# A four-layer network in one kernel: a new order of PE's work in the state-space loop, early weights for the layer behind it, and four rounds of the last attention's values moved to the sorted sparse layer's tail

## What is computed

```python
x = x + L0_xattn(ctx, layernorm(x))     # state-space scan, see below
x = x + L0_ffn(layernorm(x))            # sparse, 8 experts of which 2, and a shared one
x = x + L1_xattn(layernorm(x), ctx)
x = x + L1_ffn(layernorm(x))
x = x + L2_xattn(layernorm(x), ctx)
x = x + L2_ffn(layernorm(x))            # attention, then a sparse layer of 8 experts, sorted
x = x + L3_xattn(layernorm(x), ctx)     # 16 heads of 128; keys ctx @ Wk, values ctx @ Wv
x = x + L3_ffn(layernorm(x))
```

```python
def step(state, inp):
    d, b, c, u = inp
    dA = jnp.exp(d[..., None] * A)
    state = state * dA + (d * u)[..., None] * b[:, None, :]
    y = jnp.einsum('bdn,bn->bd', state, c)
    return (state, y)
```

```python
k = (encoder_hidden_states @ Wk).reshape(B, Skv, H, D)
v = (encoder_hidden_states @ Wv).reshape(B, Skv, H, D)
k = rmsnorm(k, gk)
```

## Time and profile before

| | |
|---|---|
| median of 3 runs | 1465.5 us (1464.37 to 1468.17) |
| the profiled execution | 1465.39 us, span 1463.5 us |
| busy, share of the span | PE 1312.8 us (90%), DVE 1022.4 (70%), ACT 707.2 (48%), POOL 270.1 (18%) |
| mean granted clock of PE | 0.947 of full speed |
| the loop of 32 steps | 41.5 to 184.1 us |
| the rest of `mamba` and the seam to `ffn0`'s first matmul | 184.1 to 204.3 us |
| blocks of `moe3` | 862 to 984.4 us |
| head of `attn4` up to its first transposes | 987.8 to 1001.0 us |

### The profile page before, as it was taken

One profiled execution on the slowest core, in us unless ns is written; L12 is line 12 of the kernel. 1 busy time (PEld: TensorE's weight loads), 2 busy tenths in 40 slices (PEclk: granted clock), 3 DMA queues, 4 the chain that ended last, 5 costly groups with the idle time before them and its releaser, 6 DMA issues.

```text
span 1463.5 us, 20903 instructions
## 1 busy us (share of the span) xinstructions
PE 1312.8 (90%) x6697; PEld 917.8 (63%) x6697; DVE 1022.4 (70%) x2266; ACT 707.2 (48%) x1824; POOL 270.1 (18%) x256
## 2 busy tenths in 40 slices
PE   7788869989998667999999799995999999989998
PEld 4354445555333244676667589984888888765555
DVE  7888777889896787887788623235666666667665
ACT  5777613443775665555554212223666666633111
POOL 0666520000000002222121173121111111201000
PEclk8899979999999769999999799997999999979999
DMA  6476640015430200000004198855222222102230
GB/s 224 153 221 214 218 180 0 1 23 94 70 56 2 83 0 1 1 37 1 37 1 131 33 348 320 305 192 180 99 72 72 72 72 72 36 1 48 79 93 29
DMA packets 82434, 141.53 MB, mean 97 GB/s; under 512 B 45493, under 2 KB 56958, under 8 KB 77008
## 3 DMA queue, kind: packets, MB, share of 16 engines
q1 hardware_dynamic: 80480, 136.28, 29.6%
q0 software_dynamic: 1872, 4.22, 0.8%
HBM read 105.06 MB, written 26.37 MB: 90 GB/s over the span
## 4 chain that ended last, share of the span: by engine, by line
PE 67%; DVE 10%; ACT 3%; issue 2%; DMA 2%; POOL 1%; SPq 0%; DVEq 0%; ACTq 0%; POOLq 0%
PE psum L3295 5%; PE psum L2496 5%; PE psum L2068 4%; PE psum L958 4%; PE psum L2792 4%; PE psum L2844 4%; PE psum L2822 4%; PE psum L2110 4%; PE psum L2857 3%; PE psum L3305 3%; PE psum L2507 2%; DVE roomB L1624 2%; PE psum L2100 2%; PE psum L2800 2%; PE psum L992 2%
## 5 line engine op out<-in xcount | busy, mean ns | idle before, releaser
L2914 ACT ACTIVATE roomA<-psum,roomA 128x256 f32<-128x256 f32 x128 | 70.9, 559 | 87.4 <-DVE roomA L2981 86.9
L2165 ACT ACTIVATE roomA<-psum,roomA 128x128 f32<-128x128 f32 (+1 forms) x128 | 53.2, 426 | 84.4 <-DVE roomA L2240 84.2
L1624 DVE TENSOR_REDUCE roomB<-psum 128x2 f32<-128x512 f32 x128 | 81.4, 686 | 8.8 <-PE psum L1463 8.2
L2031 POOL TENSOR_TENSOR roomA<-roomA 128x512 f32<-128x512 f32 x40 | 50.8, 1270 | 177.0 <-DVE roomA L2233 177.0
L875 POOL TENSOR_TENSOR roomA<-roomA 128x1024 f32<-128x1024 f32 (+1 forms) x32 | 74.5, 2328 | 48.3 <-PE psum L596 31.4
L530 PE MATMUL psum<-roomB,own 128*128 128x256 f32 x256 | 69.6, 402 | 15.2 <-ACT roomB L632 14.7
L2644 DVE SCALAR_TENSOR_TENSOR roomA<-roomA,psum 128x512 f32<-128x512 f32 x23 | 15.9, 690 | 95.5 <-ACT roomA L2543 89.4
L2068 PE MATMUL psum<-own,roomB 128*128 128x512 f32 x160 | 75.0, 594 | 3.4 <-DVE roomA L2232 2.1
L530 PEld LDWEIGHTS psum<-roomB,own 128*128 128x128 f32 x256 | 48.1, 196 | 46.1 <-ACT roomB L632 26.0
L3295 PE MATMUL psum<-roomA,roomB 128*112 128x512 f32 (+1 forms) x168 | 74.8, 593 | 0.3 <-DVE roomA L3523 0.3
L796 DVE TENSOR_TENSOR_SCAN roomA<-roomA,psum 128x512 f32<-128x512 f32 x64 | 74.4, 1204 | 0.0
(11 more groups left out here) (520 smaller groups left out, 3325.3 us busy)
## 6 DMA issues: line engine op xcount, KB each, us to landing
roomB<-m_w_dram SPq DMA_DIRECT2D x12, 1536.0 KB
roomA<-m_w_dram SPq DMA_DIRECT2D x11, 1536.0 KB
a_kv_ready<-roomB SPq DMA_DIRECT2D x32, 512.0 KB, 3.6
roomA<-m_c_rows SPq DMA_DIRECT2D x32, 512.0 KB, 4.8
roomA<-a_kv_ready SPq DMA_DIRECT2D x8, 1024.0 KB, 4.8
roomA<-a_kv_ready SPq DMA_DIRECT2D x16, 512.0 KB, 4.3
roomB<-a_w_dram SPq DMA_DIRECT2D x4, 1280.0 KB, 6.0
roomB<-f_w_dram SPq DMA_DIRECT2D x8, 624.0 KB, 4.0
```

The costliest lines, as they stand in the source:

```text
L1624: dve.tensor_reduce(maxneg[:, hp // 8, :, m, hp % 8], g.bank(m).rearrange("p (q k) -> p q k", k=S), AX.X, ALU.max, negate=True).then_inc(s ...
```

## The change

In `mamba`, the rounds in the loop fall from 26 to 22: 28 of the 32 rounds are left (`ROUNDS`), and the last four of values, pairs 6 and 7 of the heads, go to `moe3`. The steps with a round are 1 to 28 without 5, 9, 13, 17, 21 and 25. In a step PE now runs `spread`, the second half of the round that the step before began, the `add`, and then the first half of its own round. ACT's squares of a key round are cut in two fours, one behind the copy and one in the next step, behind the decay and ahead of the next copy. SP's stores come a step later. PE's last `add` stands ahead of `back(0)`. The buffer of the squares moves, so that the room from word 1200 on is free for the weights of `ffn0`; these are cut into ten loads (gate, six pieces of up, three of down), one in each step from 14 to 23, behind the row load and the store.

In `moe3`, SP loads the weights of the four late rounds with the small tables (several of the layer's semaphores are joined in one), and behind the last down matmuls PE runs the four rounds, each of four matmuls, ACT copies each and issues its store itself. The first two rounds wait for the last block's hidden values, the other two for the copies of the first two. SP waits for the four stores ahead of `attn4`'s loop.

```diff
@@ mamba
-    k_sq, k_tmp = rb.take(8, P), rb.take(3, 16 * NT)
-    rb.at = 10200
+    assert rb.at <= 1200
+    rb.at = 9176
+    k_sq = rb.take(8, P)
...
-    IN_LOOP = 32 - AHEAD
+    ROUNDS, WEIGHTS_AT = 32 - LATE_V, 14
+    IN_LOOP = ROUNDS - AHEAD
...
-    values = list(range(AHEAD)) + [AHEAD + i for i in range(IN_LOOP) if i % 13 in (1, 4, 6, 9, 11)]
-    keys = [r for r in range(32) if r not in values]
+    values = list(range(AHEAD)) + [AHEAD + i for i in range(IN_LOOP) if i % 11 in (2, 6, 9)]
+    keys = [r for r in range(ROUNDS) if r not in values]
...
             if 3 <= k + 2 < STEPS:
                 row(k + 2)
-            if k - 1 in round_at:
-                keep(round_at[k - 1])
+            if k - 2 in round_at:
+                keep(round_at[k - 2])
+            if 0 <= k - WEIGHTS_AT < g.f0_parts:
+                g.f0_part(sp, k - WEIGHTS_AT)
...
             if k + 1 < STEPS:
                 spread(k + 1)
-            if k in round_at:
-                kv_round(round_at[k], range(0, 2))
+            if k - 1 in round_at:
+                kv_round(round_at[k - 1], range(2, 4))
             if k:
                 add(k - 1)
             if k in round_at:
-                kv_round(round_at[k], range(2, 4))
-        pe.wait_ge(s["m_kv_copied"], 32)
+                kv_round(round_at[k], range(0, 2))
+        add(STEPS - 1)
+        pe.wait_ge(s["m_kv_copied"], ROUNDS)
         pe.wait_ge(s["m_products"], 2 * STEPS)
         back(0)
-        add(STEPS - 1)
         back(1)
...
+            if k - 2 in round_at and kind_of[round_at[k - 2]] == 0:
+                squares(round_at[k - 2], 1)
             if k - 1 in round_at:
-                r = round_at[k - 1]
-                kv_out(r)
-                if kind_of[r] == 0:
-                    squares(r)
+                kv_out(round_at[k - 1])
+                if kind_of[round_at[k - 1]] == 0:
+                    squares(round_at[k - 1], 0)
@@ ffn0
+    pieces = [(w_gate, d["f0_gate"])]
+    pieces += [(w_up[:, kt, e:e + 3], d["f0_up"][:, kt, e:e + 3]) for kt in range(KD) for e in range(0, E, 3)]
+    pieces += [(w_down[:, e:e + 3], d["f0_down"][:, e:e + 3]) for e in range(0, E, 3)]
+    g.f0_parts = len(pieces)
+    g.f0_part = lambda sp, i: sp.dma_start(*pieces[i]).then_inc(s["f0_weights"], 16)
...
-        sp.dma_start(w_gate, d["f0_gate"]).then_inc(s["f0_weights"], 16)
         keys.sync(sp)
-        for kt in range(KD):
-            sp.dma_start(w_up[:, kt], d["f0_up"][:, kt]).then_inc(s["f0_weights"], 16)
-        sp.dma_start(w_down, d["f0_down"]).then_inc(s["f0_weights"], 16)
...
-        pe.wait_ge(s["f0_weights"], 64)
+        pe.wait_ge(s["f0_weights"], 16 * g.f0_parts)
@@ moe3
+LATE_V = 4
...
+        sp.dma_start(v_late, d["a4_kv"].rearrange("p (n k) c -> p n k c", k=2)[:, 8 - LATE_V // 2:, 1]).then_inc(s["m3_small"], 16)
         ahead["sync"](sp)
...
+        def late_values(r):
+            if r < 2:
+                pe.wait_ge(s["m3_h"], NB)
+            else:
+                pe.wait_ge(s["m3_y"], NB + r - 1)
+            for i in range(4):
+                t = 4 * (r % 2) + i
+                ins = pe.matmul(g.ps[:, (4 + 2 * (r % 2)) * HALF + i * 2 * P:(4 + 2 * (r % 2)) * HALF + (i + 1) * 2 * P],
+                                g.CT[:, t * P:(t + 1) * P], v_late[:, r // 2, :], start=True, stop=True)
+            ins.then_inc(s["m3_up"], 1)
...
             down(b)
+        for r in range(LATE_V):
+            late_values(r)
...
+    def late_values_out(act):
+        for r in range(LATE_V):
+            act.wait_ge(s["m3_up"], NB + r + 1)
+            src = g.ps[:, (4 + 2 * (r % 2)) * HALF:(6 + 2 * (r % 2)) * HALF].rearrange("p (i q c) -> p q i c", i=4, q=2)
+            act.copy(v_staged[r % 4].rearrange("p q (i c) -> p q i c", i=4), src).then_inc(s["m3_y"], 1)
+            act.wait_ge(s["m3_y"], NB + r + 1)
+            act.dma_start(g.kv[8 - LATE_V // 2 + r // 2, 1, :, :, r % 2 * HALF:(r % 2 + 1) * HALF], v_staged[r % 4])\
+               .then_inc(s["m3_v_stored"], 16)
@@ attn4
         g.f5_first(sp)
+        sp.wait_ge(s["m3_v_stored"], 16 * LATE_V)
```

More of the change, by code:

```diff
@@ L632, in kv_out, with squares @@
             act.copy(staged[:, r % 4].rearrange("p q (i c) -> p q i c", i=4), src).then_inc(s["m_kv_copied"], 1)
-        def squares(r):
+        def squares(r, q):
             pair, half = divmod(place_of[r], 2)
@@ L2382, in moe3 @@
     v, u, hot = kept.take(NH, 2, NT), kept.take(NH, NT), kept.take(NH, NT, P)
+    v_late = kept.take(LATE_V // 2, 2 * P)
+    spare = Room(room.tensor, room.size)
+    spare.at = 17600
+    v_staged = hot.rearrange("p h i n -> p (h i n)").rearrange("p (k q t) -> p k q t", k=3, q=2)
+    v_staged = [v_staged[:, k] for k in range(3)] + [spare.take(2, HALF)]
     ahead = ffn5_ahead(g)
```

49 lines of the change are left out of this document (24 added, 25 removed).

## The result

| | before | with the change |
|---|---|---|
| median (range, runs) | 1464.93 us (1463.31 to 1468.17, 4) | 1444.28 us (1441.37 to 1446.41, 4) |
| ratio to before, 95% interval | | 0.9855 (0.9831 to 0.9879) |
| the profiled execution, span | 1465.39 us, 1463.5 | 1444.38 us, 1442.7 |
| mean granted clock of PE | 0.947 | 0.948 |

The change makes the kernel 20.7 us faster; 1442.5 had been forecast, in a range of 1436.5 to 1453. The same program run again later, beside a before of 1464.80 us, took 1446.44 (ratio 0.9874, 0.9859 to 0.9889), 18.4 us less. So 18 to 21 us is what can be said.

The account below looks back on a forecast made before the run. PE's order was taken to bound the loop where it waits, with DVE's own work the floor. From 1465.4 us: - 22.4 (loop) - 1.0 (loop's end) - 1.0 (seam) + 1.5 (tail) = 1442.5 us, range 1436.5 to 1453.

Parts of the forecast that it names:

- The loop: State-space loop: PE's new order and fewer rounds gain 22.4 us of at most 26.9, leaving 4.5; bounds 12 and 26.9.
- the heavy steps at the start: Early in the loop: three steps in a row at 3.87 us leave DVE idle 3 x 0.45 = 1.35 us.
- the balanced groups up to step 16: In the loop, PE and DVE balance within 0.1 us per four steps; small gaps of issue leave 1.0 us idle.
- The end of the loop: Last add ahead of the first half's transposes: DVE's 2.12 us wait shortens, 1.0 us gained, bounds 0.8 and 1.1.
- The early weights: Ten loads, 3.6 MB, in steps 14 to 23: a backlog of 0 to 2.4 us fits; cost 0, bounds 0 and 5.
- The seam: Into the first sparse layer: PE starts at 203.2 instead of 204.2, 1.0 us gained, bounds 0 and 1.0.
- The tail: Sorted sparse layer's end: ACT's four 512 KB stores beside the eight loads of the sums lose 1.5 us.
- ACT as the bound: Rival, 15%: in the loop, 4.49 us of ACT work per key step keeps some 12 us idle; 1450 us.
- DMA as the bound: Rival, 12%: DMA engines bound steps 14 to 23, 38.4 to 41.4 us of work for 39; five more us, 1447.5.
- Stores that cost 5.1: Rival, 10%: in the sorted layer's tail the stores hold back the sums, 5.1 us instead of 1.5; 1446 us.
- Late rows: Rival, 2%: loop rows land late, POOL, add and DVE wait; slower from landings of about 11 us, 1491 at 13.
- Order without effect: Rival, 2%: in the loop DVE waits for something behind `spread`, such as POOL's product; only seams and tail count, 1465.

Follow-up runs that it names:

- the third experiment: Changed kernel with the first sparse layer's weights loaded behind the loop in four pieces, as before: 1447.09 us, ratio 0.9872, loop 120.73 us against 120.96.
- the sixth: Changed kernel with one more 384 KB DRAM-to-DRAM copy beside each piece of weights in steps 14 to 23: 1448.67 us, loop 122.57 us.
- the seventh: Changed kernel with two more 384 KB DRAM-to-DRAM copies beside each piece of weights in steps 14 to 23: 1464.32 us in a single execution, loop 136.68 us.
- the ninth kernel: Changed kernel with nine throwaway matmuls of 512 columns behind the state-space layer's last transpose: 1439.46 us, ratio 0.9837.
- the fourth kernel: Changed kernel with the late rounds' four stores issued by SP behind its eight loads of the sums, not by ACT: 1441.87 us, later 1445.58.

## Why the prediction was right, and where it was not

**The loop: 22.4 forecast, 21.6 measured.** The reading of the timeline held: PE's order was the bound, the copy's wait went, a full step costs PE 3.88 us, and DVE is the bound now. The idle time that stays was put at 3.8 us (4.5 with the stretched steps) and is 4.15. Inside this sum the terms are off in both directions, and that the total came out is partly luck: the first wait is 1.03 us instead of 0.4 (0.57 to 1.91 in the six profiles of this loop; it was longest where the granted clock was still 0.50 until 54 us); the heavy steps at the start 1.77 (0.35, 0.54 and 0.88) instead of 1.35; the balanced groups up to step 16 leave 0.4 instead of 1.0; steps 14 to 17 0.30 instead of 1.0; behind the gates 0.65 where 0 stood. The idle time fell by 20.6 us, so that the steps' own stretch gave 1.0 us, where I had put 1.4 (2.1 less 0.7). In the second profile of the changed kernel the loop is 121.99 us, a gain of 20.6.

**The end of the loop: 1.0 forecast, 0.9 measured**, by the mechanism described.

**The early weights: 0 in the loop was right**, and the third experiment shows it. I argued from a backlog of 0 to 2.4 us; the sixth shows that there was more room than that, about one more piece a step. The queues moved 329 GB/s at a share of 0.99, and 381 when given more, and not the 309 that I had worked out from a stretch at a share of 0.69. Row landings of 5 to 7.4 us came as forecast: 5.5 in the median, and 4.3 without the weights. That POOL waits once they exceed 7.4 is borne out by the sixth and the seventh.

**The seam: 1.0 forecast as a gain, 0.1 measured as a loss in the profile of the result. This step was too simple.** "At the seam PE starts at 203.2 instead of 204.2" took two things as fixed: that the last transposed copy keeps its place, and that what is gained at the first gate matmul is kept. Measured from the last addition to X, the copy ends 11.37 us behind instead of 10.96, so the start gained 0.5; and PE, at half its clock throughout, then took 6.97 us for the gates, where the later start before had caught a stretch at 0.80 (203 to 207 us). The row that hinted at it was in front of me: a clock of 0.67 in the seam. I read it for the bandwidth alone.

One profile cannot price this piece. In the second profile of the changed kernel the gates took 4.89 us and the mark is 29.24, a gain of 1.8 and not a loss. Over all profiles without the throwaway matmuls the mark is 29.2 to 31.2 in the eight with early weights (mean 30.2) and 31.1 to 31.7 in the four with late ones (mean 31.3). So the early weights gave about 1.1 us in the mean; that this is near the forecast of 1.0 is luck, since it holds a varying clock that the forecast left out. PE's clock is worth 1.6 to 3.5 us of the seam, as the ninth kernel shows; the 8.7 us in which DVE makes the norm stay.

**The tail: 1.5 lost forecast, 1.3 measured**, and the fourth kernel takes it back. The mechanism has a part that I did not name: not only are the data's transfers shared, SP's issues themselves slow down.

**The rivals.** ACT as the bound: not with the split squares, 2.8 to 3.9 us of it with whole ones. DMA as the bound: no. Stores that cost 5.1: no. Late rows: not here, but one to two pieces a step away. Order without effect: no.

**The sum** asked for a span of 1463.5 - 22.9 = 1440.6 us, and in the first profile it is 1442.7: 0.8 more in the loop, 1.1 in the seam, 0.1 at the loop's end, 0.3 in the pieces that nothing touched, less 0.2 in the tail. The medians lie 1.8 and, the second time, 3.9 us above the forecast, both inside the range.

## What to carry to other kernels

Where an engine's step has a wait for another engine's copy in its middle, put work that does not need the copy there, and give the engine a step without the extra work now and then: the order of PE and ACT gave 16.4 us of the loop, four rounds less 5.2 more. A load moved under a loop cost nothing here while the loop's own transfers still landed within what their buffers cover (7.4 us). One more piece a step took them past that and cost 1.6 us, two more cost 15.7; find the edge by adding dummy transfers, as in experiments 6 and 7, and read landings and rates in the stretch itself, not over the whole loop. And before pricing a seam, read PE's clock in it: filling PE's idle time with matmuls that nobody reads was worth more there (1.6 to 3.5 us) than loading the weights early (1.1 in the mean).

## What the hardware did that I had not expected

- With ACT issuing four stores nearby, SP's eight issues took 7.06 us instead of 3.97, so 0.88 each instead of 0.50. Seven other runs with ACT's stores had 5.68 to 7.37; all runs with the stores on SP, or without them, had 3.97. But SP's issues get as slow without ACT where the queues are full: 3.99 us for the four stores behind the loads, up to 2.48 us for one with two extra transfers a step.
- The queues moved 307 GB/s in the changed kernel from 102 to 148 us, and 381 with one more piece a step, at a share of 1.02. The landing of a 512 KB row went from 5.5 to 7.7 and 12.0 us with one and two more, and the loop's extra length from 1.6 to 15.7 us.
- PE's granted clock is 0.50 after 8.7 us without work, and when it rises again differs between executions: the 32 gate matmuls took 3.98 to 6.97 us in eight profiles with the same seam, two of them of one program (6.97 and 4.89). A seam's length can vary by 2 us for that reason alone.
